# Probabilities and x split in SBUF and transposed by DMA in an attention and feed-forward kernel

## The chip, the core and the metric

The kernel runs on one core of a Trainium2 chip. The core has a matrix engine (TensorE, PE), a vector engine (VectorE, DVE), a scalar engine (ScalarE, ACT), a general engine (GpSimd, POOL) and a queue engine (SyncE, SP) that here issues the DMAs. Each engine works through its own instructions in order and waits on semaphores for the others. The metric is the device time of one execution in microseconds; less is better.

## What is computed

```python
# B, S, D = 8, 512, 1024; 16 heads of 64; all f32
h = layernorm(x)
q, k, v = h @ Wq, h @ Wk, h @ Wv            # rotary embedding on q and k
logits = q @ k.T / 8, causal                # for each head
x = x + layernorm(softmax(logits) @ v @ Wo)
h = layernorm(x)
y = h @ W.T + bias + lora(h)                # adapters of rank 16, one of 3 by batch
out = x + layernorm(y)
```

The results keep nearly f32 precision: each operand of a product is split into two f16 numbers, a high and a low part, and three products (high x high, high x low, low x high) are summed.

## The kernel before

After a prologue that loads and splits the weights comes the attention part, 8 batches of 8 **slots**. In slot p of batch b the kernel works on pair p of heads (two heads, a = 0 and 1): scores, softmax and the transposing of the probabilities P; it multiplies the P of the pair before with V (the PV product); and it makes q and k of the next pair and an eighth of V. Then a second part of 32 tiles does the output product, the feed-forward product and the layer norms; the change touches it only where the last weight chunks are loaded.

`over_batches` runs batch 0 and batch 7 as straight code and batches 1 to 6 in a loop of three turns with two batches each. Every engine has its own function `slot`, and the order of work on an engine is the order in which it stands there; nothing reorders it. Semaphores tie the engines.

PE in a slot (lines 503 to 543): `score_products` (L453, 24 matmuls of 128 to 512 columns, two heads side by side), the product for q (L428 to L430, 24), in p = 1 to 4 the transposes of one tile of x for the next batch (`x_transposes`, L418, 8), the product for k (24), `pv_products` of the pair before (L473), `p_transposes` (L462, 20 transposes of 128 x 128 f32 through PSUM), and `v_product` (L439 to L441, 24; not in p = 0 to 3 of batch 0 nor in p = 4 to 7 of batch 7). The scores of the next slot wait for `qk_low` of both q and k.

DVE in a slot (lines 801 to 862): eight masked scores with their row minimum (L815), the low part of V (L700), reciprocals (`inverse`, L730), `qk_drain` of q (L706, L707), statistics of the layer norm of x (L677 to L682, p = 0 to 3), the low part of x transposed (L694, p = 1 to 4), `qk_drain` of k, `qk_low_part` of q (L713), `o_evac` (L724), five `pt_evac` (L719: low part of P, from PSUM), `qk_low_part` of k, and `ln_apply` (L687, p = 0 to 3).

ACT: the high part of V (L1002), eight exponentials (L1063), the high part of x transposed (L997), `qk_high_part` of q (L1009), `o_evac` (L1018), five `pt_evac` (L1013, high part of P), `qk_high_part` of k. POOL: eight `normalise` (L1148, P times the reciprocal of the row's sum), `rotate` of q (L1139, L1141), the inverse root for the layer norm (L1135), `rotate` of k. In slot 2 of batch 7 POOL also does a reduction over partitions for Wo. So the chain from the product of k to the next scores is: drain on DVE, two rotations on POOL, high part on ACT, low part on DVE.

SP loads x for the next batch into `x_ring` (four tiles) and stores the output o of each pair. In batch 7 it loads Wo, later Wf, in four chunks of 1 MB each into `arena2`, which holds all four at once.

## Time and profile before

| | |
|---|---|
| median of 3 runs | 2287.74 us (2286.65 to 2289.22) |
| the profiled execution | 2287.41 us, its span 2285.6 us |
| PE busy | 2179.5 us, 95% of the span |
| DVE busy | 1384.5 us, 61% |
| ACT busy | 792.8 us, 35% |
| POOL busy | 774.8 us, 34% |
| attention part | 98.3 to 1509.7 us |
| mean granted clock of PE | 0.979 |

Lines of the profile name the source line of an instruction. The chain that ended last is followed back from the last instruction, at each step to what released it. A table by stretch gives, for a piece of the span, the busy time of each engine; a timeline gives instructions in order of time, like ones merged. Matmuls overlap their neighbours, so the distance between two starts says what they cost. The names `arena`, `region` and the like are buffers without their numbers.

### The profile page before, as it was taken

To read this page: it belongs to the slowest core of one execution; us is meant where nothing else is said; L and a number is where in the kernel's file an instruction comes from. 1 tells how busy PE (TensorE), PEld (TensorE's weight loads), DVE (VectorE), ACT (ScalarE), POOL (GpSimd) and SP (SyncE) were. 2 spreads that over 40 slices of the span, in tenths; PEclk is the share of its full clock that TensorE was granted. 3 is DMA by queue.
4 is the path that set the end of the run, shared out by engine and by line. 5 is a ranking of instruction groups with operands and counts; after the bars stand their busy time and mean duration, and the time that the engine had idled before them with its cause. 6 is when DMAs were issued, how large, how long until landed. Compare 5 with 4: busy or idle time off the path is not lost.

```text
span 2285.6 us, 35735 instructions
## 1 busy us (share of the span) xinstructions
PE 2179.5 (95%) x13184; PEld 1134.0 (50%) x13184; DVE 1384.5 (61%) x3327; ACT 792.8 (35%) x1829; POOL 774.8 (34%) x905
## 2 busy tenths in 40 slices
PE   3989999999999999999999998769999999999997
PEld 2445555555555555555555554434444444444443
DVE  6776676576676676576566575775555455555544
ACT  4544444444444444444444443431111111111111
POOL 0254545545455454554545544610000000000000
PEclk8999999999999999999999999879999999999999
DMA  7000010010010010000010020231121221212111
GB/s 290 2 28 15 19 42 15 20 42 10 26 42 10 24 34 19 25 29 24 16 37 24 10 88 10 85 114 63 49 93 37 93 74 48 82 38 91 38 56 37
DMA packets 31190, 108.73 MB, mean 48 GB/s; under 512 B 4161, under 2 KB 4161, under 8 KB 29986
## 3 DMA queue, kind: packets, MB, share of 16 engines
q1 hardware_dynamic: 31010, 106.34, 13.7%
q8 instruction: 112, 1.84, 0.3%
q14 instruction: 68, 0.56, 0.1%
HBM read 72.77 MB, written 33.55 MB: 47 GB/s over the span
## 4 chain that ended last, share of the span: by engine, by line
PE 91%; DVE 4%; issue 1%; POOL 1%; DMA 1%; ACT 1%; SPq 0%; POOLq 0%; DVEq 0%; ACTq 0%
PE ps L568 29%; PE ps L428 10%; PE ps L429 9%; PE ps L430 9%; PE ps L462 6%; PE ps L453 5%; PE ps L439 5%; PE ps L440 5%; PE ps L441 5%; PE ps L473 5%; PE ps L598 1%; PE ps L558 1%; PE ps L418 1%; POOL arena L1148 1%; DVE arena L719 1%
## 5 line engine op out<-in xcount | busy, mean ns | idle before, releaser
L1148 POOL TENSOR_TENSOR arena<-arena,row_inv 128x512 f32<-128x512 f32 (+3 forms) x512 | 358.3, 737 | 648.7 <-DVE row_inv L730 648.7
L428 PE MATMUL ps<-arena,region 128*128 128x512 f16 x1024 | 389.4, 380 | 0.0
L429 PE MATMUL ps<-arena,region 128*128 128x512 f16 x1024 | 388.5, 379 | 0.0
L430 PE MATMUL ps<-arena,region 128*128 128x512 f16 x1024 | 388.3, 379 | 0.0
L568 PE MATMUL ps<-region 128*128 128x512 f16 x1536 | 341.5, 383 | 8.2 <-ACT arena L1101 4.6
L815 DVE CUSTOM_DVE_ANT_0 arena<-ps,con,pow 128x512 f32<-128x512 f32 (+3 forms) x512 | 246.4, 547 | 161.5 <-PE ps L453 161.5
L568 PE MATMUL ps<-region,arena 128*128 128x512 f16 x1536 | 337.4, 379 | 0.0
L1063 ACT ACTIVATE arena<-arena,neg_max 128x512 f32<-128x512 f32 (+3 forms) x512 | 280.0, 548 | 98.3 <-DVE neg_max L815 98.3
L706 DVE TENSOR_TENSOR rotated<-ps,con 128x512 f32<-128x512 f32 x128 | 88.5, 691 | 267.2 <-PE ps L430 267.2
L568 PEld LDWEIGHTS ps<-region 128*128 128x128 f16 x1536 | 151.3, 99 | 186.5 <-issue 10.1
L568 PEld LDWEIGHTS ps<-region,arena 128*128 128x128 f16 x1536 | 149.1, 98 | 174.2 <-issue 0.8
L1009 ACT ACTIVATE qk_high<-rotated 128x512 f16<-128x512 f32 x128 | 82.6, 645 | 423.5 <-POOL rotated L1141 423.5
L881 DVE BATCH_NORM_STATS2 st<-ps 128x6 f32<-128x512 f32 x128 | 82.9, 690 | 233.1 <-PE ps L568 151.1
L1101 ACT ACTIVATE arena<-ps,sm 128x1024 f32<-128x1024 f32 x64 | 77.1, 1204 | 410.0 <-DVE sm L898 410.0
L1184 POOL TENSOR_TENSOR sm<-sm,con 128x1 f32<-128x1 f32 x64 | 35.2, 550 | 535.1 <-DVE sm L891 535.1
L439 PE MATMUL ps<-region,arena 128*128 128x512 f16 x512 | 195.3, 381 | 11.4 <-DVE region L671 11.4
L719 DVE SCALAR_TENSOR_TENSOR arena<-ps,arena 128x512 f16<-128x512 f32 x320 | 196.3, 677 | 0.0
L440 PE MATMUL ps<-region,arena 128*128 128x512 f16 x512 | 195.2, 381 | 0.0
L441 PE MATMUL ps<-region,arena 128*128 128x512 f16 x512 | 195.1, 381 | 0.0
L1139 POOL TENSOR_TENSOR swapped<-swapped,con 128x512 f32<-128x512 f32 x128 | 173.7, 1357 | 42.8 <-DVE swapped L707 35.6
L1141 POOL TENSOR_TENSOR rotated<-rotated,swapped 128x512 f32<-128x512 f32 x128 | 173.6, 1356 | 10.0
L1013 ACT ACTIVATE arena<-ps 128x512 f16<-128x512 f32 x320 | 163.4, 608 | 4.6 <-PE ps L462 4.6
(123 smaller groups left out, 2732.8 us busy)
## 6 DMA issues: line engine op xcount, KB each, us to landing
arena<-x SPq DMA_DIRECT2D x32, 512.0 KB, 3.8
...
region<-attn_scratch SPq DMA_DIRECT2D x8, 2048.0 KB, 9.1
v_split<-x SPq DMA_DIRECT2D x32, 512.0 KB, 4.2
out<-v_split SPq DMA_DIRECT2D x32, 512.0 KB, 5.1
arena<-wv SPq DMA_DIRECT2D x4, 1024.0 KB, 13.7
region<-wq SPq DMA_DIRECT2D x4, 1024.0 KB, 18.8
arena<-wk SPq DMA_DIRECT2D x4, 1024.0 KB, 6.6
```

What stands on the lines that cost most here:

```text
L428: mm(o, w[:, k, 0, cols], xnt[par][:, k, 0, :], start=(k == 0), stop=False)
L429: mm(o, w[:, k, 0, cols], xnt[par][:, k, 1, :], start=False, stop=False)
L430: last = mm(o, w[:, k, 1, cols], xnt[par][:, k, 0, :], start=False, stop=(k == KT - 1))
L439: mm(o, xnt[par][:, k, 0, tok], region[2][:, k, 0, cols], start=(k == 0), stop=False)
L440: mm(o, xnt[par][:, k, 0, tok], region[2][:, k, 1, cols], start=False, stop=False)
L441: last = mm(o, xnt[par][:, k, 1, tok], region[2][:, k, 0, cols], start=False, stop=(k == KT - 1))
L568: last = mm(ps[:, bank + c, :], stationary(k, hl), w[:, k, wl, 512 * c:512 * c + 512], start=(k == 0 and hl == 0 and wl == 0), stop=final)
L719: v.scalar_tensor_tensor(pt[:, 1, grp, :], ps[:, PT_GROUPS[grp][0], :], P_UP, pt[:, 0, grp, :], ALU.mult, ALU.subtract).then_inc(pt_low, 1)
L815: v.tensor_tensor_reduce(out=unit_sb(j, a), in0=unit_ps(j, a), in1=causal[:, 512 - width:512], scale=pow2[:, S_NEG:S_NEG + 1], scalar=HIGH ...
L1063: s.activation(unit_sb(j, a), unit_sb(j, a), ACT.Exp, bias=neg_max[:, n:n + 1], scale=-1.0, accum_out=row_sum[:, n:n + 1]).then_inc(exp_do ...
L1139: gp.tensor_tensor(swapped[which][:, :], swapped[which][:, :], sin_t, ALU.mult).then_inc(rot_mul, 1)
L1148: gp.tensor_tensor(unit_sb(j, a), unit_sb(j, a), row_inv[:, n:n + 1].broadcast_to([PART, 128 * (j + 1)]), ALU.mult).then_inc(norm_done, 1)
```

## The change

In the attention part neither P nor x goes through TensorE to be transposed.

- P: ACT multiplies the exponentials with the reciprocal of the row's sum (times 2^14) and writes the high part in f16 into `p_split` in SBUF (`p_high_part`, eight a slot, one for each unit of scores); DVE computes the low part the same way (`p_low_part`, eight). Two transposing DMAs, issued by SP, one for the high and one for the low part (each 128 partitions x 20 blocks x 128, f16, 640 KB), write `pt`. POOL's `normalise` is gone. `inverse` has a second instruction for the factor.
- x: one tile at a time (`x_tile`), normalised by DVE (`ln_apply`), high part by ACT (`xn_high_part`), low part by DVE at the start of the next slot (`xn_low_part`), and two transposing DMAs (each 128 x 8 x 128, f16, 256 KB) into `xnt`. The transposes of batch 0 before the first slot stay as they were.
- The PV product reads `pt` in the new order of blocks, in pieces of 128 or 256 columns (`PV_PIECES`): 36 matmuls with the same columns as the 24 before. The order of the score units is (2, 0, 3, 1) in place of (3, 2, 0, 1).
- On DVE `p_low_part` stands ahead of the drain of k; `ln_apply` comes right behind that drain. SP waits for `pv_done` before it issues the transposes of P, for `xn_split` before those of x.
- `pt` and `p_split` exist once. `p_split` takes room in `arena2`, so chunks 0 and 1 of Wo and of Wf are loaded a second time before they are split (`LATE_ORDER`, `raw_late`).

```diff
-Q_ORDER = (3, 2, 0, 1)
-S_OFF = {3: 0, 2: 512, 0: 896, 1: 1024}
+Q_ORDER = (2, 0, 3, 1)
+S_OFF = {2: 0, 0: 384, 3: 512, 1: 1024}
...
+PV_PIECES = {0: ((0, 2), (2, 2)), 1: ((1, 1), (2, 2)), 2: ((2, 2),), 3: ((3, 1),)}
...
+LATE_ORDER = (2, 3, 0, 1)
...
+        raw_late = [arena2[:, at:at + 2048].rearrange("p (k n) -> p k n", k=KC) for at in (4096, 6144, 0, 2048)]
+        x_tile = arena2[:, 0:1024]
+        xn_high_t = arena2[:, 1024:1536].bitcast(F16)
+        xn_low_t = sb("xn_low_t", [PART, D], F16)
+        pt = half(arena1[:, 6656:6656 + 2 * S_LEN], ("p (h n q) -> p h n q", dict(h=2, n=2 * NB)))
+        p_split = half(arena2[:, 1536:1536 + 2 * S_LEN], ("p (h a n) -> p h a n", dict(h=2, a=2)))
...
+                if not last_b and 1 <= p <= ST:
+                    tok = slice(128 * (p - 1), 128 * p)
+                    for hl, src in enumerate((xn_high_t, xn_low_t[:, :])):
+                        sp.wait_ge(xn_split[hl], n)
+                        if p == 1 and hl == 0 and not first:
+                            sp.wait_ge(qk_done[1], PAIRS * b)
+                        sp.nop(nofuse=True)
+                        sp.dma_start_transpose(xnt[1 - bp][:, :, hl, tok], src).then_inc(xnt_in[hl], 16)
                 if not last_b and p < ST:
+                    if first and p == 0:
+                        sp.wait_ge(xt_done, 2 * ST)
+                    else:
+                        need(sp, xn_split[1], n)
+                    sp.dma_start(x_tile, x_v[b + 1, p]).then_inc(x_next_in, 16)
+                if not (first and p == 0):
+                    sp.wait_ge(pv_done, g)
+                for hl in range(2):
+                    sp.wait_ge(p_done[hl], 8 * g + 8)
+                    sp.nop(nofuse=True)
+                    sp.dma_start_transpose(pt[:, hl], p_split[:, hl].rearrange("p a n -> p (a n)")).then_inc(
+                        pt_in[hl], 16)
...
-            def p_transposes():
...
-                need(pe, masked, 8 * g + 8)
-                if not last_b and 1 <= p <= ST:
-                    need(pe, xn_done, 4 * b + 4 + p)
-                    for hh in range(2):
-                        x_transposes(p - 1, hh, BANK_XT[hh])
...
                 if not (first and p == 0):
+                    need(pe, masked, 8 * g + 8)
                     need(pe, v_low, v_before(kind, p, b))
+                    for hl in range(2):
+                        need(pe, pt_in[hl], 16 * g)
                     pv_products((p - 1) % PAIRS)
-                need(pe, norm_done, 8 * g + 8)
...
-                p_transposes()
...
+            def p_low_part(g, n):
+                j, a = UNITS[n]
+                need(dve, p_done[0], 8 * g + n + 1)
+                v.scalar_tensor_tensor(unit_p(j, a, 1), unit_sb(j, a), row_inv[:, n:n + 1], unit_p(j, a, 0),
+                                       ALU.mult, ALU.subtract).then_inc(p_done[1], 1)
...
                 inverse(g, 0)
+                if not last_b and 1 <= p <= ST:
+                    xn_low_part(4 * b + p - 1)
+                inverse(g, 1)
                 if has_qk:
                     qk_drain(0, g + 1, bank)
-                inverse(g, 1)
+                need(dve, pt_in[1], 16 * g)
+                for n in range(len(UNITS)):
+                    p_low_part(g, n)
...
+            def p_high_part(g, n):
+                j, a = UNITS[n]
+                need(act, inv_done, 2 * g + 1 + n // 4)
+                s.activation(unit_p(j, a, 0), unit_sb(j, a), ACT.Copy, scale=row_inv[:, n:n + 1]).then_inc(p_done[0], 1)
+
+            def xn_high_part(n):
+                need(act, xn_done, ST + n + 1)
+                need(act, xnt_in[0], 16 * n)
+                s.activation(xn_high_t, x_tile, ACT.Copy).then_inc(xn_split[0], 1)
```

Three places show what now stands in a row. First SP, in slot 2 of a batch in the loop; the rows are its DMAs with their waits (L356 and L377 load x, L335 and L344 store o, L371 and L383 transpose). Before:

```order
L355 REGISTER_ALU
L356 ISA [waits xt_done]
L356 DMA arena<-x 128x1024
L335 ISA [waits o_low]
L335 DMA attn_scratch<-o_st 128x1024
```

Now:

```order
L367 REGISTER_ALU
L371 DMA_TRANSPOSE arena<-arena 128x8x128 [waits xn_high_done]
L371 DMA_TRANSPOSE arena<-xn_low_t 128x8x128 [waits xn_low_done]
L377 ISA [waits xn_low_done]
L377 DMA arena<-x 128x1024
L379 REGISTER_ALU
L381 ISA [waits pv_done]
L383 DMA_TRANSPOSE arena<-arena 128x20x128 [waits p_high_done]
L383 DMA_TRANSPOSE arena<-arena 128x20x128 [waits p_low_done]
L344 ISA [waits o_low]
L344 DMA attn_scratch<-o_st 128x1024
```

The load of x and the store of o are now queued with four transposes, each behind a wait of its own.

Second PE, from the PV product to the V product of a slot in which a tile of x is transposed. Before:

```order
L473 MATMUL ps<-arena,v_split 64x512 [waits v_low]
...
L473 MATMUL ps<-arena,v_split 64x128 x6
L274 REGISTER_ALU [waits norm_done]
L462 MATMUL ps<-con,arena 128x128 [waits xt_low]
L462 MATMUL ps<-con,arena 128x128 x19
L274 REGISTER_ALU
L439 MATMUL ps<-region,arena 128x512 [waits q_drained]
```

Now:

```order
L275 REGISTER_ALU [waits v_low,masked]
L507 MATMUL ps<-arena,v_split 64x256 [waits pt_low_in,pt_high_in]
...
L507 MATMUL ps<-arena,v_split 64x128 x6
L479 MATMUL ps<-region,arena 128x512 [waits q_drained]
```

The V product follows the PV product at once, and the PV product waits for both DMAs.

Third DVE, in a slot of the loop with a layer norm, from the drain of q (L706 before, L743 now) to the low part of k. Before:

```order
L707 STREAM_SHUFFLE swapped<-ps 128x512
...
L677 BN_STATS bn<-arena 128x6 [waits x_in1]
...
L694 TENSOR_TENSOR arena<-ps,arena 128x4x128 [waits xt_high]
L706 TENSOR_TENSOR rotated<-ps,con 128x512 [waits k_done]
L707 STREAM_SHUFFLE swapped<-ps 128x512
L713 TENSOR_TENSOR qk_low<-rotated,qk_high 128x512 [waits q_high]
L724 SCALAR_TENSOR_TENSOR o_st<-ps,o_st 128x512 [waits o_high]
...
L719 SCALAR_TENSOR_TENSOR arena<-ps,arena 128x512 [waits pt_high]
L713 TENSOR_TENSOR qk_low<-rotated,qk_high 128x512 [waits k_high]
L687 TENSOR_SCALAR arena<-arena,mean_var,rstd 128x1024 [waits rstd_done]
```

Now:

```order
L744 STREAM_SHUFFLE swapped<-ps 128x512
...
L275 REGISTER_ALU [waits pt_low_in]
L757 SCALAR_TENSOR_TENSOR arena<-arena,row_inv 128x384 [waits p_high_done]
...
L757 SCALAR_TENSOR_TENSOR arena<-arena,row_inv 128x256 [waits p_high_done] x2
L275 ISA
L708 BN_STATS bn<-arena 128x6 [waits x_next_in]
...
L743 TENSOR_TENSOR rotated<-ps,con 128x512 [waits k_done]
L744 STREAM_SHUFFLE swapped<-ps 128x512
L718 TENSOR_SCALAR arena<-arena,mean_var,rstd 128x1024 [waits rstd_done]
L750 TENSOR_TENSOR qk_low<-rotated,qk_high 128x512 [waits q_high]
L762 SCALAR_TENSOR_TENSOR o_st<-ps,o_st 128x512 [waits o_high]
L750 TENSOR_TENSOR qk_low<-rotated,qk_high 128x512 [waits k_high]
```

The low parts of P (L757) and `ln_apply` (L718) moved from behind the drain of k (behind its low part, for `ln_apply`) to ahead of the low part of k, the low parts of P ahead of the drain itself.

## Rows read from the trace of the kernel before

**Rows 1.** Page: busy us (share of span) x instructions; then the chain's shares.

```profile
PE 2179.5 (95%) x13184; PEld 1134.0 (50%) x13184; DVE 1384.5 (61%) x3327; ACT 792.8 (35%) x1829; POOL 774.8 (34%) x905
...
PE 91%; DVE 4%; issue 1%; POOL 1%; DMA 1%; ACT 1%; SPq 0%; POOLq 0%; DVEq 0%; ACTq 0%
```

**Rows 2.** Busy time by stretch: stretch, length, each engine, granted clock, DMA share, GB/s.

```profile
794.96:816.43 21.47, 21.47 (x142) 11.25 (x142) 15.35 (x38) 9.14 (x25) 11.32 (x13) 1.00 0.12 37
838.77:861.11 22.34, 22.34 (x150) 12.18 (x150) 15.64 (x40) 10.43 (x27) 11.37 (x13) 1.00 0.11 36
140.69:160.64 19.95, 17.23 (x124) 9.97 (x125) 15.00 (x40) 9.83 (x26) 11.38 (x13) 1.00 0.13 41
1442.18:1467.57 25.39, 18.60 (x117) 9.82 (x118) 16.51 (x34) 12.32 (x26) 14.88 (x12) 0.84 0.11 32
98.30:1509.70 1411.40, 1363.56 (x8944) 732.13 (x8944) 920.07 (x2333) 622.57 (x1649) 711.83 (x793) 0.98 0.09 30
```

**Rows 3.** Waits of PE in the attention part: us in total, times, longest.

```profile
PE ps L453 <- DVE qk_low L713: 30.1, 8, 6.2
PE ps L453 <- issue: 10.2, 3, 9.4
```

**Rows 4.** Timeline of PE in a slot: start us, us, engine line op names.

```profile
807.16 1.82 PE L473 MATMUL ps<-arena,v_split 128*64 128x512 f16 x24
808.91 2.40 PE L462 MATMUL ps<-con,arena 128*128 128x128 f32 x20
811.15 0.38 PE L439 MATMUL ps<-region,arena 128*128 128x512 f16 x1
```

**Rows 5.** Timeline of DVE in the slot from 816.43.

```profile
817.49 0.75 DVE L815 CUSTOM_DVE_ANT_0 arena<-ps,con,pow 128x512 f32<-128x512 f32 x1 [1.58 <-PE ps L453]
...
821.27 0.68 DVE L700 SCALAR_TENSOR_TENSOR v_split<-ps,v_split 128x512 f16<-128x512 f32 x1
...
823.55 0.69 DVE L706 TENSOR_TENSOR rotated<-ps,con 128x512 f32<-128x512 f32 x1 [1.51 <-PE ps L430]
...
824.88 1.25 DVE L677 BATCH_NORM_STATS2 bn<-arena 128x6 f32<-128x512 f32 x2
...
826.57 1.29 DVE L694 TENSOR_TENSOR arena<-ps,arena 128x512 f16<-128x512 f32 x2
```

**Rows 6.** Groups of ACT by line: busy us, mean ns, then idle before.

```profile
L1063 ACT ACTIVATE arena<-arena,neg_max 128x512 f32<-128x512 f32 (+3 forms) x512 | 280.0, 548 | 98.3 <-DVE neg_max L815 98.3
...
L1009 ACT ACTIVATE qk_high<-rotated 128x512 f16<-128x512 f32 x128 | 82.6, 645 | 423.5 <-POOL rotated L1141 423.5
```

**Rows 7.** Timelines of POOL and of DVE where they meet.

```profile
800.65 5.47 POOL L1148 TENSOR_TENSOR arena<-arena,row_inv 128x512 f32<-128x512 f32 x8 [10.46 <-DVE row_inv L730]
...
809.17 1.29 POOL L1139 TENSOR_TENSOR swapped<-swapped,con 128x512 f32<-128x512 f32 x1
...
809.40 1.60 DVE L713 TENSOR_TENSOR qk_low<-rotated,qk_high 128x512 f16<-128x512 f32 x1 [0.78 <-ACT qk_high L1009]
...
814.51 0.67 DVE L713 TENSOR_TENSOR qk_low<-rotated,qk_high 128x512 f16<-128x512 f32 x1
...
1452.80 4.73 DVE L671 SCALAR_TENSOR_TENSOR region<-arena,pow,region 128x2048 f16<-128x2048 f32 x2
...
1452.97 5.96 POOL L1148 TENSOR_TENSOR arena<-arena,row_inv 128x128 f32<-128x128 f32 x4 [1.51 <-DVE row_inv L730]
```

**Rows 8.** Page, DMA issues: KB each, median us to landing.

```profile
arena<-x SPq DMA_DIRECT2D x32, 512.0 KB, 3.8
...
region<-attn_scratch SPq DMA_DIRECT2D x8, 2048.0 KB, 9.1
...
arena<-wk SPq DMA_DIRECT2D x4, 1024.0 KB, 6.6
```

**Rows 9.** Timeline of SP and DVE: lora_a's issue, and the wait for bias behind it.

```profile
1502.64 0.37 SPq L340 DMA_DIRECT2D arena<-lora_a  x1
...
1508.45 0.55 DVE L795 TENSOR_REDUCE w_pmax<-arena 128x1 f32<-128x384 f32 x1 [2.25 <-DMA arena<-bias]
```

215 lines of the change are left out of this document (105 added, 110 removed), and 5 rows, old and new, of the table PT_GROUPS.

## The prediction

> **What bounds the kernel now.** I read the busy line and the chain of the page first [rows 1]: TensorE (PE) is busy for 95% of the span and makes up 91% of the chain that ended last. Then the table by stretch [rows 2]. The attention part lasts 1411.40 us, and PE is busy for 1363.56 of them. A slot (one pair of heads) takes 21.47 us without transposes of x and 22.34 us with them, PE busy for all of it, at a granted clock of 1.00. Of the 64 slots 52 are of this kind. The other 12 are four in the first batch, which have no V product (19.95 us in the row shown, of which PE works 17.23), and the eight of the last (25.39 us in the row shown, PE 18.60). There the waits of PE on `qk_low` lie [rows 3]: 30.1 us in 8 waits, and one of 9.4 us where GpSimd (POOL) stood still around its reduction. So in 52 slots work taken from PE is time gained, until another engine or a queue becomes the longest; in 12 it is not.
>
> **What leaves PE.** The transposes of P (20 in a slot) stand between the PV product and the V product [rows 4]: they start at 808.91 and the next product at 811.15, 2.24 us. The transposes of x (8 in each of four slots of every batch but the last) are the difference between the two kinds of slot, 0.87 us. The PV product becomes 36 matmuls in place of 24, with the same 7680 columns in all. Two heads run side by side, and the 24 took 1.75 us (807.16 to 808.91), 0.46 ns for each of 3840 columns: the forms of 128 columns among them cost no more than their share, so I add 0 (at most 12 more at the mean of 0.073 us: 0.9). A slot of PE alone is then 21.47 - 2.24 = 19.23, or 22.34 - 2.24 - 0.87 = 19.23 us.
>
> **What is added to the other engines,** in a slot, counted from the start of the scores. VectorE (DVE) loses five evacuations from PSUM (L719) and gets eight low parts from SBUF: two 2048-wide ones took 4.73 us (L671 [rows 7]), 1.15 ns an element, so 512, 384, 256 and 128 wide, twice each, are about 3.0 us, 3.2 with their starts (if a fixed part dominates, up to eight times 0.68, 5.4). ScalarE (ACT) loses five copies and gets eight; 512 wide is 0.65 us (L1009 [rows 6]), so all are some 3.7, less where they are short. POOL loses eight multiplications, 5.47 us [rows 7]. DVE's low parts now stand **ahead of the drain of k**, where before the evacuations stood behind it. The masked scores start 1.06 us after the scores (816.43 by the table, 817.49) and take 3.8, to 821.27 [rows 5]; with the V evacuation and the reciprocals DVE is at 5.7; q's product ends at 7.1, its drain (823.55 to the next at 824.88, a short reciprocal among it: 1.3 us) at 8.5; the high parts end at about 9.4 on ACT (eight exponentials of 0.55 on average from 1.9 on, till 6.3 [rows 6]; four high parts at once, the other four after the second reciprocal); the low parts take DVE from 8.5 to 11.7. k's product ends at 12.4, its drain at 13.7.
>
> POOL and DVE hinder each other when both read two tensors of SBUF [rows 7]: L713 took 1.60 us from 809.40 where POOL ran, 0.67 from 814.51 where it did not, and four short POOL multiplications took 5.96 us under two DVE operations back to back. So the rotation of q waits for the low parts: POOL 11.7 to 14.3. The rotation of k follows, with 0.6 us lost to `qk_low` of q, till 17.5; ACT's copy 0.65, the low part 0.67: k is ready at 18.9. PE wants it at 19.2. **Slots without x: 19.2 us, PE still the bound, with 0.3 us to spare.** In slots with a layer norm (p = 0 to 3) DVE has 1.7 us of statistics (824.88 to 826.57) ahead of k's drain, 1.2 us for the low part of x in front (p = 1 to 4), and `ln_apply`, an estimate of 0.8 by the 1024 columns, before `qk_low`: the drain ends at 14.7, POOL gives the rotation at 18.9, and k is ready at 20.2. **Those slots: 20.2 us, held by the chain through DVE and POOL**, not by PE. The clock should stay at 1.00: it was 1.00 in the slot of batch 0 where PE did nothing for 2.72 us [rows 2].
>
> **The transposing DMAs.** No row shows one, so I bound it. P goes as two transfers of 640 KB a slot, x as two of 256 KB. From below: 1024 KB land in 6.6 us and 2048 in 9.1 [rows 8], 2.5 us for 1024 KB more, so 640 KB hold the queue for 1.6 us. From above: lora_a is 1024 pieces of 192 B; from its issue at 1502.64 to the landing of what stands behind it at 1508.45 are 5.8 us [rows 9], at most 5.7 ns a piece; P in pieces of 256 B is 2560 pieces, 14.5 us. Call it t (x: 0.4 t). I take t = 3, by the row it is nearest to in bytes: of the 3.8 us in which 512 KB of x land I call 1.8 latency and 2 transfer, an estimate, so 640 KB are 2.5, rounded up because it transposes. The PV product of the slot ends at 14.1 and frees `pt`; both land at 14.1 + 2t + 1.8 = 21.9, 2.7 into the next slot. Wanted are the high one at 6.3 there (ACT overwrites the source), the low one at 8.5 (DVE), both at 12.4 (PE). So SP's waits and the stores of o behind them cost nothing up to t of about 6. The load of x is issued at 7 and landed by 12, when DVE asks for it at 11.7: hidden up to about 0.3.
>
> The Trainium skill (DMA: Bandwidth & Descriptors, "Latency and other measured facts") gives 261 GB/s for a transposing DMA with a middle dimension that is not contiguous. By that, an estimate from the page, 640 KB would take 2.5 us and the sum would stay as it is; no run here shows it.
>
> **The sum.** Batches 1 to 6: 4 x 22.34 + 4 x 21.47 = 175.2 us now; p = 0 to 3 at 20.2 and p = 4 to 7 at 19.2 are 157.6; gain 17.6, in six batches 106. Batch 0, p = 4 to 7: 22.34 + 3 x 21.47 - 4 x 19.2 = 10. Batch 0, p = 0 to 3: 19.95 now, 20.2 by the chain, -1. Last batch: p = 0 and 3 win about 2 each; p = 1 and 2, where two weight maxima stand on DVE ahead of k's drain together with the low parts, lose about 3 together (an estimate); p = 4 to 7 stay bound by DVE and POOL: about 0 in sum. The second loading of two weight chunks lies beside the attention output product. Together 115 us: 2285.6 - 115 = 2170.6 of span; the profiled run took 2287.41 beside its span and the median is 2287.74, so 2.1 more: **2173 us.**
>
> **The rivals.**
> *1, DVE and POOL cost more.* If POOL gets in between the low parts each time (one of its operations is 1.3 us [rows 7]), or a low part has a larger fixed cost, DVE's part ahead of k's drain grows by 1.3 (one POOL operation) to 2.5 us (two), and all 52 slots end some 1 to 2 us later: 2225, between 2200 and 2250. For it speaks the slack of only 0.3 us; against it that DVE's back-to-back operations were not interrupted [rows 7].
> *2, the transposes are somewhat slower,* t from 5 to 7. They reach the point where DVE waits for `pt_low_in` ahead of k's drain, and the load of x stands behind them in the queue. The gain melts: 2200 to 2283; at t of about 7 nothing is left.
> *3, the queue of transposes becomes the bound: slower than before.* `pt` and its source are single. Then a slot is both P transfers, latency, and the PV product between: 2t + 1.8 + 1.9 = 2t + 3.7, with x 2.8t + 3.7. A batch is 19.2 t + 29.6, against 175.2: it decides from t = 7.6 (with DVE's wait included, from about 7). At t = 10 a batch takes 222, 46 more, in 7.5 batches 350: some 2640. At the upper bound 14.5 it is 308, 1000 us more, 3290. For it: the elements change partition one by one, which no copy of this trace does. Against: nothing but the plain rows.
> The Trainium skill has a rule that speaks for it (VectorE: DVE Perf Modes, "The three transpose paths"): 1309 ns for one 128 x 128 block by DMA against 390 on TensorE. Were the 20 blocks one after another, this estimate would give t = 26 us, beyond rival 3's bound; no row bears it out.
>
> **Chances.** Forecast, 2150 to 2200: 0.42. Below: 0.02. Rival 1: 0.12. Rival 2: 0.08. Within 0.2% (4.6 us, about what a measurement of this kernel can tell from no change): 0.04. Rival 3 up to 2650: 0.15; beyond: 0.17. Faster 0.64, same 0.04, slower 0.32. The range 2150 to 2650 holds 0.81; the likeliest case's own is 2150 to 2200.
>
> **What would show it.** Right: slots of 19.2 us for p = 4 to 7 with PE busy throughout, 20.2 for p = 0 to 3 with PE waiting for `qk_low` of k for about 1 us; DMA issues of P that land in 4 to 8 us. Rival 1: the waits on `qk_low` in every slot. Rivals 2 and 3: PV matmuls that wait for the DMA, DVE's first low part waiting for it. Wrong altogether would be PV matmuls slower per column.

## The result, and the profile after

The changed kernel takes **2321.45 us** (median; 2320.89 to 2325.9) against 2287.19 us for the kernel before in the same comparison: a ratio of 1.0153, with a 95% interval of 1.0136 to 1.0171. It is 34 us slower, where 2173 us, 115 us faster, was forecast. The forecast's direction was wrong; the range of 2150 to 2650 holds the time.

The page of the profiled execution first: busy time of the engines, the chain that ended last by engine, and what TensorE (PE) waited for in the attention part (us in total, times, longest).

```profile
span 2319.1 us, 34896 instructions
...
PE 2057.9 (89%) x12448; PEld 1017.2 (44%) x12448; DVE 1584.2 (68%) x3619; ACT 871.7 (38%) x1993; POOL 461.8 (20%) x393
...
PE 49%; issue 20%; DVE 15%; POOL 11%; ACT 3%; DMA 1%; DVEq 0%; POOLq 0%; SPq 0%; ACTq 0%
```

```profile
PE ps L493 <- DVE qk_low L750: 166.6, 55, 11.1
PE ps L493 <- issue: 20.1, 9, 9.8
```

Against [rows 1] PE is busy for 122 us less, so the transposes did leave it. Its share of the chain fell from 91% to 49%, VectorE (DVE) with GpSimd (POOL) now hold 26%, and 20% is "issue", time in which the engine on the chain waited for nothing that the profile shows. PE waits for `qk_low`, the low part of k, ahead of the scores in 55 of 64 slots, 166.6 us together; before it was 8 slots and 30.1 us [rows 3].

The table by stretch (length, busy time of each engine, granted clock, DMA share, GB/s) answers to [rows 2]. The first row is a slot without a layer norm (p = 7), the next three are p = 1, 2 and 3 of the next batch, the last is p = 4. The norm stands in p = 0 to 3, and I call those x slots.

```profile
787.50:807.68 20.18, 19.32 (x132) 9.61 (x133) 15.22 (x38) 10.53 (x28) 5.89 (x4) 1.00 0.39 80
830.03:852.37 22.34, 19.32 (x133) 9.66 (x133) 19.59 (x44) 11.48 (x29) 6.88 (x5) 1.00 0.55 118
852.37:876.35 23.98, 20.96 (x133) 10.34 (x134) 19.63 (x44) 11.48 (x29) 6.89 (x5) 0.93 0.56 109
876.35:900.32 23.97, 20.95 (x133) 10.32 (x133) 19.63 (x44) 11.48 (x29) 6.89 (x5) 0.93 0.52 111
900.32:922.10 21.78, 20.91 (x132) 10.25 (x133) 16.26 (x39) 10.54 (x28) 5.89 (x4) 0.92 0.39 72
```

The reader is to see two losses. At a clock of 1.00 PE works for 19.32 us, near the forecast 19.23, and then stands still for 0.86 us in a p = 7 slot and for 3.02 us in an x slot. And from the third x slot of this batch on, PE's own busy time is 1.6 us longer, at a granted clock of 0.92 to 0.93.

**Where the first loss arises** stands in the timelines of DVE, POOL and PE in the slot from 787.50 (start, us; the bracket is the idle time before). L757 are the eight low parts of P, L743/L744 the drain of k, L1185/L1187 the two operations of a rotation, L750 a low part of q or k.

```profile
795.87 5.80 DVE L757 SCALAR_TENSOR_TENSOR arena<-arena,row_inv 128x384 f16<-128x384 f32 x8
801.59 0.68 DVE L743 TENSOR_TENSOR rotated<-ps,con 128x512 f32<-128x512 f32 x1
...
806.66 0.69 DVE L750 TENSOR_TENSOR qk_low<-rotated,qk_high 128x512 f16<-128x512 f32 x1 [2.57 <-ACT qk_high L1049]
```

```profile
796.06 1.54 POOL L1185 TENSOR_TENSOR swapped<-swapped,con 128x512 f32<-128x512 f32 x1 [10.29 <-DVE swapped L744]
797.68 1.46 POOL L1187 TENSOR_TENSOR rotated<-rotated,swapped 128x512 f32<-128x512 f32 x1
...
803.00 1.62 POOL L1185 TENSOR_TENSOR swapped<-swapped,con 128x512 f32<-128x512 f32 x1 [3.86 <-DVE swapped L744]
804.70 1.26 POOL L1187 TENSOR_TENSOR rotated<-rotated,swapped 128x512 f32<-128x512 f32 x1
```

```profile
799.70 1.84 PE L507 MATMUL ps<-arena,v_split 128*64 128x256 f16 x36
...
807.68 0.34 PE L493 MATMUL ps<-qk_high 64*128 64x384 f16 x2 [0.86 <-DVE qk_low L750]
```

POOL got in between the low parts, with both operations of q's rotation. The product of k had ended at 799.7, where PE goes on to PV, but DVE came to its drain only at 801.59, and from there drain, rotation, ScalarE's copy and low part follow one another to 807.35. In an x slot the same happens, and statistics and `ln_apply` stand in that path too. This is `qk_low` of q there, with POOL's L1185 running from 847.23 to 848.96:

```profile
847.04 0.80 DVE L718 TENSOR_SCALAR arena<-arena,mean_var,rstd 128x1024 f32<-128x1024 f32 x1
...
847.76 1.75 DVE L750 TENSOR_TENSOR qk_low<-rotated,qk_high 128x512 f16<-128x512 f32 x1
```

**Where it does not arise: the transposing DMAs.** SyncE's timeline and the DMA issues (median us to landing), which no row of before could show:

```profile
801.71 6.20 SPq L383 DMA_TRANSPOSE arena<-arena  x2
```

```profile
arena<-arena SPq DMA_TRANSPOSE x156, 4.9
arena<-xn_low_t SPq DMA_TRANSPOSE x28, 3.1
```

Two transfers of 640 KB hold SyncE for 6.20 us, 3.1 each. (The row of 156 counts the 128 transfers of P and the 28 of x's high part together.) No wait of PE, DVE, ScalarE or POOL between 98 and 1500 us ends on a DMA.

By part of the program, from the starts of the slots in both traces: batch 0 lost 6.5 us, batches 1 to 6 lost 10 (1052 to 1062), batch 7 11.4 up to its last slot, and the stretch from the last slot's scores to the end 5.8. Less the 0.2 us by which the first slot starts earlier, this is 33.5, the difference of the spans.

### The profile page after: what moved, and what is told of

The parts are those of the page before. It is cut to its first block, busy times and chain, and to the rows that moved or that the text cites. A ratio compares the mean times of both kernels' runs of the same rounds, so it can differ in the third digit from the quotient of the medians.

```text
span 2319.1 us, 34896 instructions
## 1 busy us (share of the span) xinstructions
PE 2057.9 (89%) x12448; PEld 1017.2 (44%) x12448; DVE 1584.2 (68%) x3619; ACT 871.7 (38%) x1993; POOL 461.8 (20%) x393
## 4 chain that ended last, share of the span: by engine, by line
PE 49%; issue 20%; DVE 15%; POOL 11%; ACT 3%; DMA 1%; DVEq 0%; POOLq 0%; SPq 0%; ACTq 0%
PE ps L598 28%; DVE arena L757 8%; POOL swapped L1185 6%; POOL rotated L1187 5%; PE ps L493 4%; PE ps L468 3%; PE ps L469 3%; PE ps L470 3%; DVE bn L708 2%; ACT arena L1109 1%; PE ps L628 1%; PE ps L588 1%; DVE w_part L658 1%; PE ps L479 1%; PE ps L481 1%
## 5 line engine op out<-in xcount | busy, mean ns | idle before, releaser
L468 PE MATMUL ps<-arena,region 128*128 128x512 f16 x1024 | 397.0, 388 | 0.4 <-DVE v_split L737 0.4
L469 PE MATMUL ps<-arena,region 128*128 128x512 f16 x1024 | 394.2, 385 | 0.0
L470 PE MATMUL ps<-arena,region 128*128 128x512 f16 x1024 | 392.2, 383 | 0.7 <-issue 0.7
L1185 POOL TENSOR_TENSOR swapped<-swapped,con 128x512 f32<-128x512 f32 x128 | 204.9, 1601 | 897.7 <-DVE swapped L744 890.7
L757 DVE SCALAR_TENSOR_TENSOR arena<-arena,row_inv 128x384 f16<-128x384 f32 (+3 forms) x512 | 369.2, 789 | 0.2 <-ACT arena L1054 0.2
L1109 ACT ACTIVATE arena<-arena,neg_max 128x384 f32<-128x384 f32 (+3 forms) x512 | 280.0, 548 | 143.0 <-DVE neg_max L854 143.0
L854 DVE CUSTOM_DVE_ANT_0 arena<-ps,con,pow 128x384 f32<-128x384 f32 (+3 forms) x512 | 246.4, 547 | 99.5 <-PE ps L493 89.4
L493 PE MATMUL ps<-qk_high 64*128 64x384 f16 (+3 forms) x512 | 92.6, 354 | 186.7 <-DVE qk_low L750 166.6
L1054 ACT ACTIVATE arena<-arena,row_inv 128x384 f16<-128x384 f32 (+3 forms) x512 | 237.5, 546 | 0.0
L750 DVE TENSOR_TENSOR qk_low<-rotated,qk_high 128x512 f16<-128x512 f32 x128 | 118.2, 923 | 131.5 <-ACT qk_high L1049 131.5
L479 PE MATMUL ps<-region,arena 128*128 128x512 f16 x512 | 195.9, 383 | 11.4 <-DVE region L702 11.4
L1187 POOL TENSOR_TENSOR rotated<-rotated,swapped 128x512 f32<-128x512 f32 x128 | 183.7, 1435 | 10.0
L468 PEld LDWEIGHTS ps<-arena,region 128*128 128x128 f16 x1024 | 101.3, 99 | 138.4 <-issue 27.4
```

Source lines behind the costliest of these rows:

```text
L468: mm(o, w[:, k, 0, cols], xnt[par][:, k, 0, :], start=(k == 0), stop=False)
L469: mm(o, w[:, k, 0, cols], xnt[par][:, k, 1, :], start=False, stop=False)
L470: last = mm(o, w[:, k, 1, cols], xnt[par][:, k, 0, :], start=False, stop=(k == KT - 1))
L479: mm(o, xnt[par][:, k, 0, tok], region[2][:, k, 0, cols], start=(k == 0), stop=False)
L757: v.scalar_tensor_tensor(unit_p(j, a, 1), unit_sb(j, a), row_inv[:, n:n + 1], unit_p(j, a, 0), ALU.mult, ALU.subtract).then_inc(p_done[1], 1)
L854: v.tensor_tensor_reduce(out=unit_sb(j, a), in0=unit_ps(j, a), in1=causal[:, 512 - width:512], scale=pow2[:, S_NEG:S_NEG + 1], scalar=HIGH ...
```

## The experiments

My theory: POOL and DVE take turns instruction by instruction where both read two tensors in SBUF, so that the low parts lose 2 to 2.6 us to q's rotation (step 1). The norm's place adds up to 2.2 us in x slots (step 2). PE's waits of 3 us then bring its clock down, for 1.6 us more (step 3). The rivals: low parts that are slow by themselves, a norm that costs the same anywhere, scores that are slow without the clock, and a DMA queue near its limit. Kernels that leave out part of the computation say so.

### The rotation of q behind the low parts

```
                 if has_qk:
+                    pool.wait_ge(p_done[1], 8 * g + 8)
                     rotate(0, g + 1)
```

> GpSimd's rotation of q waits for the eight low parts of P of its slot. Theory 1 (VectorE and GpSimd take turns, one instruction each, and the low parts lost 2.6 us a slot to the two rotation instructions): the eight low parts fall from 5.8 to 3.2-3.9 us, k is drained 2 us earlier; the rotation of q now comes behind them, so k's rotation queues behind q's on GpSimd and only part of the 2.6 us comes back: slots p=5-7 from 20.2 to 19.3-19.9, slots with x (p=0-3) from 23.3 on average to about 21-22, whole 2255 (2235-2290). Theory 2 (the low parts are slow for a reason of their own: ScalarE's writes or the transposing DMAs reading the same tile): they stay near 5.8 us, GpSimd starts 3-4 us later for nothing, whole 2400 or more.

Measured: **2219.44 us** (2218.97 to 2219.93), ratio to the kernel before 0.9698 (0.9682 to 0.9714), 102 us less than the changed kernel. One added wait turns the loss into a gain. Outside the turns of the loop, p = 5 to 7 take 19.55 to 19.65 us, as expected; most x slots take 20.45, less than the 21 to 22 expected, and the whole lies below the expected range. The groups of DVE by form show it best (busy us, mean ns). First the changed kernel, then this one:

```profile
L757 DVE SCALAR_TENSOR_TENSOR arena<-arena,row_inv 128x384 f16<-128x384 f32 x128 | 136.3, 1107 | 0.2 <-ACT arena L1054 0.2
L757 DVE SCALAR_TENSOR_TENSOR arena<-arena,row_inv 128x128 f16<-128x128 f32 x128 | 102.3, 837 | 0.0
...
L757 DVE SCALAR_TENSOR_TENSOR arena<-arena,row_inv 128x512 f16<-128x512 f32 x128 | 89.8, 740 | 0.0
...
L757 DVE SCALAR_TENSOR_TENSOR arena<-arena,row_inv 128x256 f16<-128x256 f32 x128 | 55.6, 473 | 0.0
```

```profile
L757 DVE SCALAR_TENSOR_TENSOR arena<-arena,row_inv 128x512 f16<-128x512 f32 x128 | 90.1, 746 | 0.0
L757 DVE SCALAR_TENSOR_TENSOR arena<-arena,row_inv 128x384 f16<-128x384 f32 x128 | 72.4, 607 | 0.2 <-ACT arena L1054 0.2
L757 DVE SCALAR_TENSOR_TENSOR arena<-arena,row_inv 128x256 f16<-128x256 f32 x128 | 56.0, 478 | 0.0
L757 DVE SCALAR_TENSOR_TENSOR arena<-arena,row_inv 128x128 f16<-128x128 f32 x128 | 38.9, 346 | 0.0
```

The widths 384 and 128 come first in the order of the units, and they run while POOL rotates q: 1107 and 837 ns against 607 and 346 without POOL. The widths 512 and 256 come last, when POOL is done, and are the same in both kernels. Each width occurs twice in a slot, and of each early pair one instruction loses about 1.0 us: 2.0 us a slot, which is q's rotation. Theory 2 (slow by themselves) falls.

### The rotations on 64 columns

Leaves out seven eighths of each rotation; order and waits are those of the changed kernel.

```
-                gp.tensor_tensor(swapped[which][:, :], swapped[which][:, :], sin_t, ALU.mult).then_inc(rot_mul, 1)
+                gp.tensor_tensor(swapped[which][:, 0:64], swapped[which][:, 0:64], sin_t[:, 0:64], ALU.mult).then_inc(rot_mul, 1)
...
-                gp.tensor_tensor(rotated[which][:, :], rotated[which][:, :], swapped[which][:, :],
+                gp.tensor_tensor(rotated[which][:, 0:64], rotated[which][:, 0:64], swapped[which][:, 0:64],
```

> Leaves out part of the computation: in each slot GpSimd's two rotation instructions work on 64 of the 512 columns. Order and waits are as in the changed kernel. Theory 1: low parts at 3.2-3.9 us for eight, the low part of q in the x slots back at 0.65 instead of 1.76 us, and k's chain shorter by 2.5 us more; every slot bound by TensorE (19.2-19.5), granted clock 1.00 throughout, whole 2150-2180. Theory 2: the low parts stay at 5.8 us for eight and only GpSimd's own 2.5 us go: p=5-7 19.3, p=0-3 about 21.3, whole 2215-2235. The group of the low parts tells the two apart: mean 400-490 ns or 780.

Measured: **2148.87 us** (2147.76 to 2150.99), a ratio of 0.9391 (0.9376 to 0.9407). The mean of the low parts falls from 789 to 555 ns, with no wait added. The slots are PE's own:

```profile
724.28:743.53 19.25, 19.25 (x133) 9.53 (x133) 15.73 (x43) 11.48 (x29) 3.09 (x5) 1.00 0.50 109
743.53:762.79 19.26, 19.26 (x135) 9.53 (x134) 16.83 (x44) 11.48 (x29) 3.10 (x5) 1.00 0.68 138
```

POOL's work alone separates 2321 from 2149; that holds both what it took from DVE and its own time in k's rotation, and the low parts' mean tells of the first. Theory 2's 2215 to 2235 is excluded. The mean of 555 ns is above the 490 that I had expected, though: also alone the eight low parts are longer than I took them for (3.8 us from first to last, against 3.2).

### The layer norm of x behind k's drain

```
                     qk_drain(1, g + 1, 1 - bank)
                 if not last_b and p < ST:
-                    ln_apply(p, 4 * b + 4 + p, x_tile)
+                    need(dve, x_next_in, 16 * (4 * b + p + 1))
+                    ln_stats(p, 4 * b + 4 + p, x_tile)
                 if has_qk:
                     qk_low_part(0, g + 1)
...
                     qk_low_part(1, g + 1)
+                if not last_b and p < ST:
+                    ln_apply(p, 4 * b + 4 + p, x_tile)
```

POOL's power stands behind `rotate(1)`, ScalarE's high part of x behind that of k; the statistics' old place ahead of k's drain is empty.

> The layer norm of x (statistics 1.7 us, the power on GpSimd, apply 0.8 us, ScalarE's high part) goes behind k's drain, k's rotation and both low parts of q and k. Theory 1 for the x slots (p=0-3 are 3.1 us longer than p=5-7 by the norm's 2.5 us ahead of q's low part, and from the third on by half clock for the scores): p=0-3 fall from 22.4/24.0 to 20.2-20.6, the granted clock stays at 1.00 in them, whole 2225-2245. The low parts of P stay at 5.8 us. Rival (the norm is paid wherever it stands, because VectorE holds up k's rotation on GpSimd): p=0-3 at 21.5-22.3, whole 2270-2290.

Measured: **2227.86 us** (2227.24 to 2229.34), a ratio of 0.9738 (0.9721 to 0.9754), 94 us less than the changed kernel. The low parts stay at a mean of 789 ns, as expected. The x slots are now as long as the others and, but for the first behind each of the two turns of the loop (21.7 and 21.9 us at 0.93 and 0.92), at full clock:

```profile
775.21:795.44 20.23, 19.32 (x132) 9.64 (x133) 19.41 (x45) 11.38 (x29) 6.50 (x5) 1.00 0.61 132
795.44:815.66 20.22, 19.33 (x133) 9.67 (x133) 19.38 (x45) 11.38 (x29) 6.50 (x5) 1.00 0.63 129
```

DVE's busy time hardly moves (19.59 to 19.41 us). What counted was only what stood between k's product and k's low part. The rival (the norm costs the same anywhere) falls.

### Both edits

> The edits of the two before together. If the low parts lose to GpSimd's interleaving and the x slots to the norm's place: all slots of batches 0-6 at 19.3-20.0, clock 1.00, whole 2180-2215, below the kernel before. If GpSimd's chain (two rotations of 2.9 us, each behind the other and behind the low parts) is then the bound: slots at 20.2-20.8, whole 2240.

Measured: **2184.43 us** (2182.78 to 2185.84), a ratio of 0.9546 (0.953 to 0.9561). Slots in batches 1 to 6 take 19.55 to 19.65 us, x or not, except for one or two at each turn of the loop over batches (21 to 22). This is near the 2173 forecast for the change as it stood. The gains of the single edits, 102 and 94 us, do not add up (137 together): each one alone already takes back most of the clock's share, and of the 2.8 us by which an x slot now becomes shorter at full clock (22.35 to 19.57) the first edit alone takes 1.9 and the second 2.1.

### Filling PE's wait

```
+                need(pe, masked, 8 * g)
+                if not last_b and 1 <= p <= ST:
+                    for k in range(10):
+                        mm(ps[:, 3, :], region[0][:, k % KT, 0, 0:128], xnt[bp][:, k % KT, 0, :], start=True, stop=True)
                 need(pe, qk_low[0], g + 1)
                 need(pe, qk_low[1], g + 1)
-                need(pe, masked, 8 * g)
```

> The changed kernel with ten matmuls of 128 columns... each 512 columns wide (about 2.1 us, results unused, later overwritten by the scores) placed on TensorE between the V product and the wait for q and k, in slots p=1 to 4 of batches 0 to 6. Nothing else moves and the wait is 3 us long in the slots behind an x slot, so they delay nothing at full clock. Theory (the idle 3 us let the clock fall to its lower level, and the scores then take 3.3 instead of 1.8 us): slots p=2,3 from 23.98 to 22.35, p=4 from 21.8 to 20.2, granted clock of these slots 1.00, whole 2321 minus 28 to 40, about 2287. Rival (the 1.6 us are not the clock but the scores waiting for something else, or the fall comes from the score phase itself): slots stay at 23.98, whole 2321 or somewhat above.

Measured: **2281.14 us** (2279.22 to 2282.06), a ratio of 0.997 (0.9959 to 0.9982): 40 us less than the changed kernel, by adding work. Contrary to the expectation one thing did move: the wait for `masked` now stands ahead of those for `qk_low`, in every slot. The granted clock is 1.00 in these slots (x slots, and p = 4 in the second row), where it was 0.92 to 0.93:

```profile
852.70:874.79 22.09, 21.48 (x142) 10.62 (x143) 19.59 (x44) 11.48 (x29) 6.89 (x5) 1.00 0.57 121
874.79:894.90 20.11, 19.33 (x132) 9.64 (x133) 16.24 (x39) 10.54 (x28) 5.89 (x4) 1.00 0.43 81
```

So the 1.6 us a slot were the clock, in its lower level of the two (1.2 GHz), and the fall came with the idle time ahead of the scores: in the unfilled kernel the scores from 852.37, behind a 3.01 us wait, last until the product for q starts at 855.60, 3.2 us; at full clock they take 1.7. The rival falls. Of the 40 us, 34 are the clock's: in the unfilled kernel 21 slots of batches 1 to 6 were longer by 1.63 us at the lower level. The other slots, at full clock in both kernels, became 0.1 to 0.25 us shorter too (22.35 to 22.10 for x slots, 20.19 to 20.10 for p = 5 to 7); whether the moved wait does that was not tested.

### Half as much again on the transposing queue

```
+        spare = sb("spare", [PART, 5, PART], F16)
...
                     sp.wait_ge(p_done[hl], 8 * g + 8)
+                    need(sp, spare_in, 16 * (4 * g + 2 * hl + 0))
+                    sp.nop(nofuse=True)
+                    sp.dma_start_transpose(spare[:, :, :], con[:, 128:448].bitcast(F16)).then_inc(spare_in, 16)
...
                     sp.dma_start_transpose(pt[:, hl], p_split[:, hl].rearrange("p a n -> p (a n)")).then_inc(
                         pt_in[hl], 16)
+                    need(sp, spare_in, 16 * (4 * g + 2 * hl + 1))
+                    sp.nop(nofuse=True)
+                    sp.dma_start_transpose(spare[:, :, :], con[:, 128:448].bitcast(F16)).then_inc(spare_in, 16)
```

> The changed kernel with one more transposing DMA of 128x640 f16 from a constant tile into a spare one ahead of each of P's two in every slot, and one behind (four of 5 blocks where P has two of 20: half as much again on the queue, and 2 to 3 us more until P's low half has landed). Theory (P's copies have room; nothing that TensorE waits for comes from a DMA inside the batches): slots unchanged within 0.1 us, whole 2321-2330. Rival (the queue is close to being the bound, or its traffic in SBUF is what lengthens VectorE's and GpSimd's instructions): PV waits for the copies, or the low parts of P rise above 789 ns, whole 2350 or more.

Measured: **2329.67 us** (2326.54 to 2331.83), 8 us more than the changed kernel. This is the edge of what the theory gave and far from the rival's 2350. The ordinary slots are unchanged (20.2, 22.35, 23.97), and so are the low parts, by form (1135 against 1107 ns for the widest change, 473 and 473 for the least). DMA's share rises:

```profile
q1 hardware_dynamic: 595042, 251.10, 48.8%
```

The profiled execution is 10.9 us longer than that of the changed kernel. 4.0 of them lie behind the start of the last slot, where PE's last PV now waits 15.3 us for P's transfers (10.40 us for O's bank in the changed kernel); p = 1 of batches 4 and 6 now runs at the lower clock and takes 1.65 us more each; and the three slots around each of the two turns of the loop (p = 7, 0 and 1) take 0.6 and 1.2 us more together. The first slot behind a turn is 2.9 and 2.5 us longer (26.7 and 26.6 us), but the slot ahead of it is 1.5 shorter both times, so most of that is only moved. Around the turns the engines show idle time that ends on "issue", up to 7.1 us for PE's weight loads; whether the DMA traffic has a part in it no run separates. So the copies have room in the batches, and none in the last slot.

### The last batch

On top of both edits, in the last batch: GpSimd's reduction of Wo's maximum behind k's rotation, the partial maxima and low parts of Wo and Wf behind k's drain and behind k's low part, and in the last slot `o_evac` and `clear_lora` ahead of Wf's partial maxima.

```
+                if last_b and p == PAIRS - 1:
+                    o_evac(g - 1, (p - 1) % 2)
+                    clear_lora()
+                if has_qk:
+                    qk_drain(1, g + 1, 1 - bank)
                 if last_b and p in (1, 2):
                     part_max(W_O, 2 * (p - 1))
...
+                if has_qk:
+                    rotate(1, g + 1)
+                if last_b and p == 2:
+                    weight_max(W_O, 1)
```

> The kernel with both edits (2184) and, in the last batch, the weights' work taken out of the way of q and k: Wo's maximum over partitions on GpSimd behind k's rotation (it now keeps k's rotation waiting 12.8 us once), Wo's and Wf's partial maxima and low parts on VectorE behind k's drain and behind the low part of k, and in the last slot the evacuation of O and the clearing of the LoRA tiles ahead of Wf's partial maxima. Expected: slot p=2 from 34.4 to 23-25, p=1 and p=6 1-3 us less, the wait of the last PV for O's bank from 10.4 to about 2: whole 2155-2168. If the all-reduce then holds up q's rotation of the next slot instead (13.8 us of GpSimd against some 11 us until it is due), p=3 takes 3-4 us of that back: 2168-2174.

Measured: **2154.42 us** (2153.56 to 2155.13), a ratio of 0.9419 (0.9404 to 0.9435), 133 us below the kernel before and just under the expected range. p = 2 takes 20.2 us in place of 34.4, where 23 to 25 were expected. The reduction came with 5.9 us of issue time and cost p = 3 nothing (19.3 us), so the second warning in the expectation did not come true. In the last slot the wait changed its name. PE's timeline:

```profile
1356.21 2.46 PE L507 MATMUL ps<-arena,v_split 128*64 128x256 f16 x36 [2.62 <-DVE neg_max L854]
1369.28 3.41 PE L507 MATMUL ps<-arena,v_split 128*64 128x256 f16 x36 [10.62 <-DMA arena<-arena]
1381.11 12.21 PE L598 MATMUL ps<-region 128*128 128x512 f16 x48 [8.41 <-DMA region<-attn_scratch]
```

The last PV no longer waits for O's bank (10.40 us in the changed kernel) but 10.62 us for P through the DMAs: masks, exponentials, low parts, then two transfers. The last slot has no products to hide them behind. It is the one place where PE waits for the transposing DMAs in this kernel.

### The load of O first

```
+                if last_b and p == PAIRS - 1:
+                    sp.wait_ge(qk_done[1], PAIRS * B)
+                    for a in range(2):
+                        sp.wait_ge(o_stored[a], 16 * PAIRS)
+                    load_o(0, 0)
```

> The kernel of the run before (2154) with one transfer moved: in the last slot of the last batch SyncE issues the load of O of batch 0 (2048 KB, 9 us) before it waits for P of that slot, instead of behind P's transposing DMAs, the store of O and the LoRA loads. Expected if the second part starts late because this load is queued late: the first product of the second part no longer waits 8.4 us for it, P's copies land as before, whole 2144-2149. Rival (the load delays P's transposing DMAs of the last slot, which the last PV already waits 10.6 us for): that wait grows by 3-9 us and the whole stays at 2150-2156.

Measured: **2154.98 us** (2152.85 to 2155.4), a ratio of 0.9417 (0.9401 to 0.9432): no gain. The rival was right, although the wait grew by 2.6 us and not by 3 to 9. The 8.41 us wait for the load is gone, but P's two transfers hold SyncE for 8.65 us in place of 6.27, the last PV waits for 13.18 us, and the LoRA loads behind them come 2.4 us later, counted from the start of the slot. On the chain of what ended last, the load of the bias is followed by DVE's work for LoRA and by the second product of the second part, which waits 10.54 us:

```profile
1362.64 8.65 SPq L384 DMA_TRANSPOSE arena<-arena  x2
```

```profile
1373.23 3.17 PE L508 MATMUL ps<-arena,v_split 128*64 128x256 f16 x36 [13.18 <-DMA arena<-arena]
1397.41 3.17 PE L599 MATMUL ps<-region 128*128 128x512 f16 x7 [10.54 <-ACT arena L1153]
```

The start of the second part hangs on the whole queue, not on this one transfer.

### How VectorE and GpSimd share: four more kernels

[Rows 7] had led me to believe that GpSimd does not get in between DVE's instructions, and in the kernel with both edits this is so in two places, of which this is the first: two low parts of Wo (2048 columns each) and POOL's first operation behind them, DVE's row and POOL's.

```profile
1316.17 4.61 DVE L702 SCALAR_TENSOR_TENSOR region<-arena,pow,region 128x2048 f16<-128x2048 f32 x2
```

```profile
1316.34 5.57 POOL L1185 TENSOR_TENSOR swapped<-swapped,con 128x512 f32<-128x512 f32 x1 [13.71 <-DVE arena L757]
```

[Rows 7] itself does not say the same. Its rows merge like instructions; taken singly, in the kernel before, they are these, DVE's two and the first of POOL's four:

```profile
1452.80 2.33 DVE L671 SCALAR_TENSOR_TENSOR region<-arena,pow,region 128x2048 f16<-128x2048 f32 x1
1455.04 2.49 DVE L671 SCALAR_TENSOR_TENSOR region<-arena,pow,region 128x2048 f16<-128x2048 f32 x1
```

```profile
1452.97 2.42 POOL L1148 TENSOR_TENSOR arena<-arena,row_inv 128x128 f32<-128x128 f32 x1 [1.51 <-DVE row_inv L730]
```

POOL's multiplication (0.40 us where DVE does not hold it up) ended at 1455.39, 0.26 us behind DVE's first low part, and DVE's second took 2.49 us in place of 2.34. So POOL had got in between the two, at a small price, as its operation is short. The same stands at 1427 us.

So what makes the low parts of P different from the pair at 1316 us: the waits between them, or their length? Two kernels tried each by itself, on the changed kernel.

One wait for all eight:

```
-                need(dve, p_done[0], 8 * g + n + 1)
...
+                dve.wait_ge(p_done[0], 8 * g + 8)
                 for n in range(len(UNITS)):
                     p_low_part(g, n)
```

> The changed kernel, in which VectorE waits once for all eight high parts of P and then runs the eight low parts with no wait between them (before, each waits for its own high part). Question: in the kernel before, and in the one with both edits, GpSimd did not get in between two low parts of Wo that stood back to back (4.6 us for two, GpSimd's operation held up for 5.6 us); between the low parts of P it does. If the wait between the instructions is the opening: the eight low parts now run uninterrupted in 3.7-3.9 us, mean 540 ns, starting up to 0.7 us later, GpSimd's first rotation operation takes 4-5 us, and the whole is 2240-2300. If not: low parts 5.8 us again, mean about 790 ns, whole 2320-2340.

Two instructions of 1280 columns:

```
-                for n in range(len(UNITS)):
-                    p_low_part(g, n)
+                dve.wait_ge(p_done[0], 8 * g + 8)
+                for a in range(2):
+                    v.scalar_tensor_tensor(p_split[:, 1, a, :], scores[:, a, :], row_inv[:, a:a + 1], p_split[:, 0, a, :],
+                                           ALU.mult, ALU.subtract).then_inc(p_done[1], 4)
```

> Leaves out part of the computation: the eight low parts of P are two instructions of 1280 columns, each with the row factor of one unit only (the other units' low parts are wrong in value); one wait ahead of both. Same elements as before. If the length of the instruction decides, so that GpSimd gets no turn between long ones as between the low parts of Wo: 2.9-3.1 us for both, means about 1490 ns. If GpSimd gets its turn between any two: one rotation operation, 1.0-1.3 us, lies between them, 4.0-4.3 us for both, mean about 2100 ns; the second operation of the rotation comes behind them. Whole 2190-2260 in both cases.

Measured: **2340.22 us** (2337.11 to 2349.32; a ratio of 1.0239, 1.0216 to 1.0261) and **2284.06 us** (2282.16 to 2285.14; 0.9979, 0.9969 to 0.9989). Neither expectation fits and neither kernel settles the question: DVE now started 1.4 us later, POOL's first operation ran in that gap, and only the second met DVE. With one wait the eight took 4.80 us, one of POOL's operations (1.0) more than the 3.8 alone; the two long ones took 4.11 against 3.0, but POOL's operation had started as they began, not between them. So two more kernels release POOL only when the first instruction has ended, into the middle of the second.

```
                 if has_qk:
+                    pool.wait_ge(p_done[1], 8 * g + 1)     (eight instructions; 8 * g + 2 with four long ones)
                     rotate(0, g + 1)
```

> The whole computation, in the order of the changed kernel: the eight low parts stand behind one wait for all high parts, with no wait between them, and GpSimd's rotation of q is released when the first low part has ended. It comes into the second. If a wait between VectorE's instructions is what lets GpSimd in, the eight take 3.7-3.9 us. If GpSimd gets its turn anyway, both its operations lie among them: 5.7-6.0 us, mean about 780 ns, whole 2340-2370.

> Leaves out and doubles part of the computation: four low parts of 1280 columns each (1.48 us alone, the second pair a repetition of the first), one wait on ScalarE ahead of them, and GpSimd's rotation of q released when the first of them has ended, so that its first operation comes into the second. If long instructions of VectorE keep GpSimd out: 5.8-6.0 us for the four, and 4-5 us for GpSimd's first operation, as between the two low parts of Wo in the kernel with both edits. If GpSimd gets its turn behind the instruction that runs when it asks: both its operations lie among the four, 7.8-8.4 us for them, mean about 2000 ns, each operation of GpSimd 1.5-2.7 us. The whole is not of interest (about 2340 to 2400).

Measured in one execution each, so that only the durations count: 2390.04 us for the eight (2340 to 2370 was expected), 2540.55 us for the four long ones (these do the low parts twice). The eight took 5.88 us and the four 7.95, both as expected if POOL gets its turn anyway. By form in the kernel with eight, and the timelines in the one with four (DVE, then POOL):

```profile
L756 DVE SCALAR_TENSOR_TENSOR arena<-arena,row_inv 128x128 f16<-128x128 f32 x128 | 170.7, 1372 | 0.0
...
L756 DVE SCALAR_TENSOR_TENSOR arena<-arena,row_inv 128x384 f16<-128x384 f32 x128 | 73.0, 611 | 38.7 <-ACT arena L1054 38.7
```

```profile
804.61 7.95 DVE L872 SCALAR_TENSOR_TENSOR arena<-arena,row_inv 128x1280 f16<-128x1280 f32 x4
```

```profile
806.30 2.43 POOL L1189 TENSOR_TENSOR swapped<-swapped,con 128x512 f32<-128x512 f32 x1 [14.22 <-DVE arena L872]
808.81 2.39 POOL L1191 TENSOR_TENSOR rotated<-rotated,swapped 128x512 f32<-128x512 f32 x1
```

With POOL asking during the second of the eight, it is now the two of 128 columns, third and fourth, that pay: 1372 ns against 346, 1.03 us each, and those of 384 columns are back at 611. No wait stands between them. Of the four long ones two pay 1.0 us (1531 ns at least, 2566 at most), and each of POOL's operations waits for the rest of one of DVE's. In that kernel a wait, met long before, stands ahead of the third and of the fourth. So POOL gets its turn behind whichever instruction runs when it asks: without a wait between at 128 and 384 columns, with one at 1280. Why the pairs of Wo's low parts in the kernel with both edits let POOL in only behind the second stays open. A wait stands ahead of each of them too, and their length alone cannot be it, as the same pair let POOL in before the change. What differs is POOL's operation, a rotation of 512 columns in place of a multiplication of 128, and no run varied it.

## Why the prediction was wrong, step by step

**What leaves PE: right.** A slot of PE alone is 19.25 to 19.32 us; 19.23 was forecast. The PV product of 36 matmuls takes 1.84 us from its start to the end of its last (799.70), against 1.82 for 24 [rows 4]; adding 0 held.

**The transposing DMAs: right.** t = 3 was forecast, 3.1 came. Rivals 2 and 3, which had 0.40 of the chances, did not occur in the batches. The estimate from the Trainium skill (DMA: Bandwidth & Descriptors, "Latency and other measured facts") was 2.5 us; SyncE's row says 3.1, some 210 GB/s. The 1309 ns that the Trainium skill (VectorE: DVE Perf Modes, "The three transpose paths") gives for one block cannot be multiplied by the number of blocks, as the prediction tried: with 20 blocks in a transfer, 3.1 us are 155 ns a block.

**The failed step: "So the rotation of q waits for the low parts".** I read [rows 7] as showing that back-to-back operations of DVE are not interrupted, and used this twice: for the low parts in 3.2 us, and against rival 1. It does not hold. Behind the instruction of DVE that runs when POOL asks, POOL's operation starts, and DVE's next one waits until it has ended: twice 1.0 us. That makes 5.80 us for the eight instead of 3.2, of which 0.6 are my own term for them, too small even without POOL (3.8 measured). The row that I leaned on does not show it either: it adds up like instructions, and taken singly POOL's first multiplication had come in between DVE's two (the rows from 1452.80 above). It cost DVE 0.15 us there and was lost in the sum of 4.73; a rotation costs 1.0. I also carried the row over to instructions of 128 to 512 columns without a row of that size.

The Trainium skill (SBUF — State Buffer, "SBUF: two separate sides") says that a DVE instruction with two inputs in SBUF and a GpSimd instruction that reads SBUF lock each other out, and that whichever starts first keeps the ports "for the whole instruction". The forms agree for the low parts of P: an instruction that meets POOL's loses 1.0 us, the others nothing. The pair of Wo's low parts at 1316 us is not explained by it: the second started while POOL was waiting.

The consequences ran as the prediction's own clock of a slot has them. k's drain ended 15.4 us into the slot and not at 13.7 (802.9 less 787.50). k was ready at 19.85 and not at 18.9. PE started at 20.18, not 19.2. **Rival 1 named the mechanism and the price (2.5 us for both operations) but not its weight.** It gave 2225, and it had 0.12. It counted 1 to 2 us a slot and left out the two terms below.

**x slots: the term was too small.** Forecast 20.2; 22.35 at full clock. The 2.6 us of the low parts come on top of the statistics, and `qk_low` of q meets POOL (1.75 us for 0.68), which holds k's rotation up once more. The first run above removed the low parts' share (22.35 to 20.45), the third the norm's (to 20.2).

**"The clock should stay at 1.00": wrong.** I took this from one slot of batch 0 with 2.72 us of idle time. Here the scores from 830.03, behind 3.02 us of waiting, still ran at the upper level (1.7 us), and those from 852.37, behind 3.01 more, at the lower (3.2 us); so did those of the next two slots. One slot that keeps its clock did not show what the same wait does slot after slot, and the trace of before had the answer two slots on. PE waited 2.72, 2.72 and 2.71 us ahead of p = 2, 3 and 4 of batch 0; the third time its scores ran at the lower level. These are the first matmuls of p = 3 and of p = 4:

```profile
160.64 0.39 PE L453 MATMUL ps<-qk_high 64*128 64x512 f16 x2 [2.72 <-DVE qk_low L713]
180.59 0.61 PE L453 MATMUL ps<-qk_high 64*128 64x512 f16 x2 [2.71 <-DVE qk_low L713]
```

That slot took 23.90 us at a granted clock of 0.93, where the prediction's sum counts it as 22.34. In the changed kernel the clock costs 34 us in batches 1 to 6 (21 slots of 1.63), as much as the whole regression; the filled variant gives them back.

**The sum.** For batches 1 to 6, 157.6 us a batch was forecast; 177.0 came. The 19.4 are: p = 5 to 7, 1.0 each; p = 4, 1.0; four x slots, 2.15 each; and the clock, 1.63 in 21 slots of the six batches, 5.7 a batch. That makes 18.3, the rest lies at the turns of the loop. Batch 0 was to win 9 and lost 6.5; its p = 0 to 3, forecast at 20.2 each, took 23.7 to 23.9 at a granted clock of 0.79 to 0.86. Six batches and batch 0 are thus 132 of the 149 us between forecast and result.

**Last batch and tail: sized at zero, worth 17.** Batch 7 lost 11.4 us in slots that I had called bound by DVE and POOL anyway: if so, work added to DVE ahead of k's drain counts in full. Keeping POOL out of the low parts (the first run) gives 7.5 of them back. The tail lost 5.8. "The second loading of two weight chunks lies beside the attention output product" missed what is new in the last slot: the last PV waits 10.40 us for O's evacuation, P comes through the DMAs, and the LoRA loads are queued behind them. The first product of the second part then waits 8.68 us for its load, against 3.54 before.
